# Four graph layers on one core: sixty edge columns listed at the first joint, three per relational group, twenty in a later node step

## The chip, the cores and the metric

One Trainium2 chip, one of its cores. The metric is the device time of one launch in microseconds, lower is better.

## What is computed

A graph of 3125 nodes with 128 features and 53125 directed edges, sorted by destination. Four layers follow each other, each wrapped as `x = layernorm(x + layer(x))`:

```python
# L0: five attention convolutions: per edge alpha = q[dst].k[src], softmax over the edges of one dst, sum of v[src]
# L1: one relational layer: softmax per (edge type, dst), sum of the weighted rows
# L2: two GCN layers: out = segment_sum(h[src] * dinv[src] * dinv[dst], dst) + b, elu between them
# L3: edge-weighted sum, and here the roles are turned round:
h = node_features @ weight
msg = edge_val[:, None] * h[edge_col]                     # edge_col is dst
out = jax.ops.segment_sum(msg, edge_row, num_segments=n)  # edge_row is src
```

The edges come sorted by destination, and L3 adds up by source. So the kernel must sort them once by source.

## The kernel before, in words

The edges are laid out as 416 columns of 128 (T = 416), in 13 groups (GROUPS) of 32 columns. Every edge pass goes through the groups in order. GpSimd (POOL) starts one indirect DMA per column, which fetches the rows of 128 edges from a table in DRAM (`gather_group`, L620), into one of two buffers per group parity. TensorE, VectorE and ScalarE work on the group before. A pass ends with a drain of some twelve turns, in which the other engines finish and POOL has no more gathers.

The passes in order: five attention convolutions (layers 0 to 4; layers 1 to 3 are one hardware loop), the relational pass (`rel_edges`), two GCN passes (`plain_edges`, tags g1_ and g2_) and the source-sorted pass (`list_edges`, tag s_). Between them stand node steps: `conv_next` (the joint behind layers 0 to 3), `last_joint` (behind layer 4), the block of n1 (`norm_joint`, behind the relational pass), the block of e1 (`elu_joint`, between the two degree passes g1 and g2) and that of n2. Each of these stages is a block: all engines leave it together, and the next begins.

**The edge list.** Layer 0's pass also ranks the edges by the block of their source. VectorE's last step (`placed`) gives each edge its place, and SP writes the places to DRAM (`ord_tab`, L973). From then on the list `lst_tab` can be filled: `order_in` (L627 and L628, two DMAs) loads some columns of places and of edge data (`ord_now`, `pay`), and `list_rows` (L634) starts one indirect DMA per column on POOL, which scatters 128 entries of 16 bytes. The 416 columns are spread over the program by hand, as `LISTED` says. Before the change:

```python
JOINT = 34; MID = 26; PER = MID + JOINT; DRAIN = 30; EACH = 6; BEHIND_REL = 50
LISTED = [JOINT + (CONVS - 2) * PER, DRAIN + 28, EACH * (GROUPS - 1), BEHIND_REL + 22]
```

So it lists 34 columns in the first joint, 26 in the drain and 34 in the joint of each of layers 1 to 3, 30 in the drain of layer 4 and 28 in the last joint, 6 behind the gathers of each of the first twelve relational groups, 50 behind the last relational gather and 22 in n1's block. The joints, the last joint and n1's block wait for the semaphore `listed`, that is until the entries have landed; the drains don't. Pass g2 loads the whole list (L2097).

Names used below. In the relational pass, VectorE's `leak` (L1750) is the first instruction that reads a gathered group: it waits for all 32 gathers of the group. `weigh` (L1724) is the last that reads the group's rows, and POOL may fill a buffer again when the `weigh` of the group two before is done.

Of the kernel before, what the change touches and what calls it, by code (L numbers as in the profile page):

```python
# [26 lines left out]
CONVS = 5  # L27
# [3 lines left out]
GROUPS = -(-EDGES // (P * TG))  # L31
T = GROUPS * TG
# [5 lines left out]
JOINT = 34  # L38
MID = 26
PER = MID + JOINT  # L40
DRAIN = 30
EACH = 6
BEHIND_REL = 50
LISTED = [JOINT + (CONVS - 2) * PER, DRAIN + 28, EACH * (GROUPS - 1), BEHIND_REL + 22]
MOST = 72
TW = 26
assert sum(LISTED) == T
NT = NPAD // P
# [4 lines left out]
def gnn_kernel(nc, xT_in, src_c, edges_c, dst_c, dst_row, prev_row, next_row, first_row, first_next, last_row,  # L53
# [14 lines left out]
    ord_tab = nc.dram_tensor("ord_tab", [P, T], i32).ap()  # L68
# [5 lines left out]
    def sem(name):  # L74
        if name not in sems:
            sems[name] = nc.alloc_semaphore(name)
        return sems[name]
# [11 lines left out]
    def settle(eng):  # L89

        eng.sem_inc(sem(f"settled_{eng.engine.name}"), 1)
# [22 lines left out]
    with root:  # L114
# [16 lines left out]
        ord_now = gsb("ord_now", [P, MOST], i32)  # L131
        pay = gsb("pay", [P, MOST, 4], i32)
# [492 lines left out]
        def order_in(eng, first, count, there="ord_in"):  # L625

            eng.dma_start(ord_now[:, 0:count], ord_tab[:, ds(first, count)]).then_inc(sem(there), 16)  # L627
            eng.dma_start(pay[:, 0:count, :], edges_c[:, ds(first, count), :]).then_inc(sem(there), 16)  # L628

        def list_rows(pool, count, since=0):  # L630


            for i in range(since, since + count):
                nc.gpsimd.indirect_dma_start(  # L634
                    lst_tab, bass.IndirectOffsetOnAxis(ap=ord_now[:, i:i + 1], axis=0), pay[:, i, :], None
                ).then_inc(sem("listed"), 16)
# [112 lines left out]
        def conv_next(l, nx, acc, sb, pb):  # L749
# [14 lines left out]
            with nc.Block() as block:  # L764
                @block.gpsimd
                def _(pool):
                    pool.wait_ge(sem("ord_in"), 32 * (l + 1))
                    settle(pool)
                    list_rows(pool, JOINT, 0 if isinstance(l, int) else MID)
                    pool.wait_ge(sem("listed"), 16 * PER * l + 16 * JOINT)  # L770
                    settle(pool)

                @block.sync
                def _(sp):
                    if isinstance(l, int):
                        order_in(sp, 0, JOINT)
                    store_rows(sp, l + 1, stage)

                @block.tensor
# [95 lines left out]
        def conv_edges(l, sb, pb, acc, deg=None, kv=None, fetch=None, nx=None, rank=None):  # L875
# [45 lines left out]
            with nc.Block() as block:  # L921
                @block.gpsimd
                def _(pool):
                    gather_all(pool, lambda g, par: gather_group(pool, tag, l, g, par, kv_tab, src_all, kv), since)
                    if rank is None:
                        pool.wait_ge(sem("ord_in"), 32 * (l + 1))
                        if not isinstance(l, int):
                            settle(pool)
                        list_rows(pool, MID if deg is None else DRAIN)

                @block.sync
                def _(sp):
                    def scatter_rows(g, par):
                        sp.dma_start(st8[:, par, :].bitcast(u8), st_tab[ds(g * P, P), :]).then_inc(sem(f"{tag}st_in{par}"), 16)

                    def sum_rows(g, par):
                        sp.dma_start(s8[:, par, :].bitcast(u8), s_tab[ds(g * P, P), :]).then_inc(sem(f"{tag}s_in{par}"), 16)

                    def group(g, par):
                        for q in range(QG):  # L940
                            n = quad(g, q)
                            at = bases(sp, g * TG + 4 * q)
                            if not skip(g):
                                sp.wait_ge(sem(tag + "qx"), n - QG + 1)
                                settle(sp)
                            for j in range(4):
                                sp.dma_start(qwin[:, q, j, :], q_tab[ds(at[j], P), :]
                                             ).then_inc(sem(f"{tag}qwin{q}"), 16)
                            if q == 1 and not skip(g):
                                if not (isinstance(g, int) and g < 3):  # L950
                                    sp.wait_ge(sem(tag + "S"), quad(g - 2, 0))
                                    settle(sp)
                                sum_rows(g - 1, 1 - par)
                            if q == 4 and not (isinstance(g, int) and g == LAST):
                                if not skip(g):
                                    sp.wait_ge(sem(tag + "ST"), quad(g, 0))
                                    settle(sp)
                                scatter_rows(g + 1, 1 - par)
                    scatter_rows(0, 0)
                    fetch(sp)  # L960
                    for g in range(3):
                        group(g, g % 2)
                    with sp.Fori(1, (GROUPS - 1) // 2 - 1) as k:
                        group(2 * k + 1, 1)
                        group(2 * k + 2, 0)
                    group(LAST - 1, 1)
                    group(LAST, 0)
                    sp.wait_ge(sem(tag + "S"), quad(LAST - 1, 0))
                    settle(sp)
                    sum_rows(LAST, 0)  # L970
                    if rank is not None:
                        sp.wait_ge(sem("k_placed"), 4)
                        sp.dma_start(ord_tab, r_i).then_inc(sem("k_out"), 16)  # L973
                        sp.wait_ge(sem("k_out"), 16)

                @block.tensor
                def _(pe):
# [266 lines left out]
        def conv_layer(l, name, nx, first=False):  # L1244
            with ExitStack() as keep:
                wide = maker(keep, nc.sbuf_tensor, name)
                kv = wide("kv", [P, 2 * TG, 2 * D]) if first else None
                if first:
                    with ExitStack() as part:
                        conv_project(nx, maker(part, nc.sbuf_tensor, name), maker(part, nc.psum_tensor, name))  # L1250
                    tables(kv)
                acc = wide("acc", [P, NPAD + P])

                def fetch(sp):
                    if not first:
                        order_in(sp, l * PER - MID, PER)
                    load_next(sp, l + 1, nx)
                    sp.dma_start(nx["ln"][:, :], col0[ds(l, 1), :, :].rearrange("l p n -> (l p) n")
                                 ).then_inc(sem("nx_cols"), 16)
                with ExitStack() as part:  # L1260
                    conv_edges(l, maker(part, nc.sbuf_tensor, name), maker(part, nc.psum_tensor, name), acc, None, kv, fetch, nx,
                               nx if first else None)
                with ExitStack() as part:
                    conv_next(l, nx, acc, maker(part, nc.sbuf_tensor, name + "_n"), maker(part, nc.psum_tensor, name + "_n"))
# [608 lines left out]
        def norm_joint(tag, acc, rs, sb, pb, loads, w, put, scale_n=None, pre=None, shift=None, aside=None, lists=False):  # L1873
# [17 lines left out]
            with nc.Block() as block:  # L1891
                if lists:
                    @block.gpsimd
                    def _(pool):
                        list_rows(pool, LISTED[3] - BEHIND_REL, BEHIND_REL)
                        pool.wait_ge(sem("listed"), 16 * T)

                @block.sync
                def _(sp):
# [274 lines left out]
        def elu_joint(tag, acc, y, w, bias, dinv_f, dinv_n, sb, pb):  # L2174
# [7 lines left out]
            stage = sb("stage", [P, 3, 4, D])  # L2182
            pp = [pb(f"pp{i}", [P, 4, D]) for i in range(4)]
            with nc.Block() as block:
                @block.sync
                def _(sp):
                    store_staged(sp, tag, stage, put_rows)
# [43 lines left out]
        def last_layers(dinv_f, dinv_n, rs):  # L2231
# [4 lines left out]
            with ExitStack() as keep:  # L2236
                wide = maker(keep, nc.sbuf_tensor, "_g")
                acc, y = wide("acc", [P, NPAD]), wide("y", [P, NPAD])
                wa, wb, wc = (wide(k, [P, D]) for k in ("wa", "wb", "wc"))
                bias = [wide(f"bias{i}", [P, 3]) for i in range(3)]  # L2240
# [7 lines left out]

                scope, sb, pb = part("g1_")
                with scope:  # L2250
                    plain_edges("g1_", CONVS + 1, acc, sb, pb, [(wa[:, :], w2[0]), (wb[:, :], w2[1]), (bias[0][:, :], b2[0])],
                                Head("g1_", acc, rs, diag, (wa, xT, dinv_f)))
                scope, sb, pb = part("e1_")
                with scope:
# [11 lines left out]
                scope, sb, pb = part("g2_")  # L2266
# [5 lines left out]
                scope, sb, pb = part("n2_")  # L2272
# [14 lines left out]
                scope, sb, pb = part("s_")  # L2287
                with scope:
                    list_edges(lst, dst_i, own, start_i, acc, sb, pb, Head("s_", acc, rs, diag))
                scope, sb, pb = part("n3_")  # L2290
# [127 lines left out]
        with ExitStack() as scope:  # L2418
# [3 lines left out]
            with ExitStack() as part:  # L2422
                deg = part.enter_context(nc.sbuf_tensor("deg", [1, NPAD + P], f32))
# [61 lines left out]
```

## Time and profile before

| | |
|---|---|
| median of 3 runs | 5692.46 us (5691.00 to 5696.89) |
| profiled execution | 5703.85 us, of which the span is 5702.0 us |
| busy share: PE, PEld, DVE, ACT, POOL | 64%, 51%, 59%, 27%, 71% |
| POOL instructions | 4168, of which 3744 gathers (L620) and 416 lists (L634) |
| mean granted TensorE clock | 0.689 of full speed |

Times in the rows are microseconds from the start of the span, durations in microseconds; the mean of a group is in ns. PE is TensorE's matmul, PEld its weight load, DVE VectorE, ACT ScalarE, POOL GpSimd, SP the DMA-issuing queue. A row of the timeline tells its start, its duration, the engine, the line, the operation, its output and inputs, and in brackets how long the engine was idle before and what ended that.

### The profile page before, as it was taken

To read this page: it belongs to the slowest core of one execution; us is meant where nothing else is said; L and a number is where in the kernel's file an instruction comes from. 1 tells how busy PE (TensorE), PEld (TensorE's weight loads), DVE (VectorE), ACT (ScalarE), POOL (GpSimd) and SP (SyncE) were. 2 spreads that over 40 slices of the span, in tenths; PEclk is the share of its full clock that TensorE was granted. 3 is DMA by queue.
4 is the path that set the end of the run, shared out by engine and by line. 5 is a ranking of instruction groups with operands and counts; after the bars stand their busy time and mean duration, and the time that the engine had idled before them with its cause. 6 is when DMAs were issued, how large, how long until landed. Compare 5 with 4: busy or idle time off the path is not lost. (4 is left out here: it accounts for less than half of the span.)

```text
span 5702.0 us, 84663 instructions
## 1 busy us (share of the span) xinstructions
PE 3639.0 (64%) x17936; PEld 2902.4 (51%) x17937; DVE 3386.0 (59%) x9194; ACT 1523.1 (27%) x3590; POOL 4073.0 (71%) x4168
## 2 busy tenths in 40 slices
PE   5767767666676756666888857777444444446556
PEld 3556546563565445654666546667333333343334
DVE  7777756665666646665666567777434343436665
ACT  4333324332343323332455522332100010000000
POOL 4477577776777777776777677777677767767775
PEclk6777777777677767776899955555655555557777
DMA  7656266554565275644656443331121121112111
GB/s 240 173 169 188 81 202 185 173 156 125 175 189 170 82 207 170 186 131 145 181 171 181 113 92 72 76 72 38 50 52 53 52 62 52 52 48 57 52 53 51
DMA packets 631577, 681.11 MB, mean 119 GB/s; under 512 B 178674, under 2 KB 512952, under 8 KB 631144
## 3 DMA queue, kind: packets, MB, share of 16 engines
q0 software_dynamic: 166480, 384.69, 24.2%
q1 hardware_dynamic: 464792, 293.16, 17.6%
q8 instruction: 93, 1.52, 0.1%
q14 instruction: 212, 1.74, 0.1%
HBM read 620.51 MB, written 56.89 MB: 119 GB/s over the span
## 5 line engine op out<-in xcount | busy, mean ns | idle before, releaser
L620 POOL DMA_INDIRECT kvconv<-kv_tab,src_all x1664 | 1627.2, 978 | 644.4 <-issue 498.5
L620 POOL DMA_INDIRECT rowsg_<-h_tab,src_all x832 | 789.8, 949 | 287.4 <-issue 252.9
L634 POOL DMA_INDIRECT lst_tab<-pay,ord_now x416 | 429.0, 1031 | 223.5 <-issue 124.6
L620 POOL DMA_INDIRECT rows_r<-rel_tab,idx_r x416 | 417.0, 1002 | 143.2 <-issue 123.4
L620 POOL DMA_INDIRECT rowss_<-h_tab,dst_i_g x416 | 398.3, 957 | 161.7 <-issue 121.9
L620 POOL DMA_INDIRECT kvlast<-kv_tab,src_all x416 | 410.0, 986 | 133.7 <-issue 121.9
L1063 ACT ACTIVATE Sconv<-s8conv 128x512 f32<-128x512 fp8e4 x384 | 240.8, 627 | 396.6 <-PE pA1conv L1021 288.8
L1125 DVE TENSOR_TENSOR msgconv<-kvconv,sm_attEconv 128x512 f32<-128x512 f32 x416 | 285.8, 687 | 84.0 <-PE pA1conv L1021 32.9
L1021 PEld LDWEIGHTS pA0conv<-Sconv,msgconv 128*128 128x128 f32 x1664 | 299.8, 254 | 13.5
L1021 PEld LDWEIGHTS pA1conv<-Sconv,msgconv 128*128 128x128 f32 x1664 | 290.4, 246 | 16.9
L1021 PE MATMUL pA0conv<-Sconv,msgconv 128*128 128x128 f32 x1664 | 298.5, 339 | 0.0
L1150 DVE TENSOR_REDUCE sm_alphaconv<-prodbconv 128x16 f32<-128x512 f32 x416 | 283.1, 681 | 2.4 <-DVE sm_exconv L473 0.5
L1021 PE MATMUL pA1conv<-Sconv,msgconv 128*128 128x128 f32 x1664 | 281.3, 326 | 0.0
L1053 ACT ACTIVATE STconv<-st8conv 128x512 f32<-128x512 fp8e4 x416 | 257.8, 628 | 84.1 <-DMA st8conv<-st_tab 79.0
L1609 PEld LDWEIGHTS pA_r<-S_r,msg_r 128*128 128x128 f32 x832 | 199.1, 329 | 9.4
L998 PE MATMUL pQ0conv<-qwinconv,STconv 128*128 128x128 f32 x832 | 146.8, 332 | 86.3 <-DMA qwinconv<-q_tab 84.2
L1609 PE MATMUL pA_r<-S_r,msg_r 128*128 128x128 f32 x832 | 199.0, 421 | 0.0
L2130 DVE TENSOR_SCALAR Sg_<-iota_row,rel_nowg_ 128x128 f32<-128x128 f32 x832 | 185.2, 315 | 9.3 <-DVE rel_nowg_ L641 4.8
L1616 PEld LDWEIGHTS pn_r<-last_now_r,msg_r 128*128 128x128 f32 x832 | 189.9, 333 | 0.0
L998 PEld LDWEIGHTS pQ0conv<-qwinconv,STconv 128*128 128x128 f32 x832 | 128.6, 235 | 106.2 <-DMA qwinconv<-q_tab 58.6
L998 PE MATMUL pQ3conv<-qwinconv,STconv 128*128 128x128 f32 x832 | 180.2, 388 | 2.1 <-ACT STconv L1053 1.1
L1616 PE MATMUL pn_r<-last_now_r,msg_r 128*128 128x4 f32 x832 | 177.5, 336 | 0.0
(655 smaller groups left out, 8961.6 us busy)
## 6 DMA issues: line engine op xcount, KB each, us to landing
qwinconv<-q_tab SPq DMA_DIRECT2D x1664, 64.0 KB
kvconv<-kv_tab,src_all POOLq DMA_INDIRECT x1664
st8conv<-st_tab SPq DMA_DIRECT2D x52, 512.0 KB
s8conv<-s_tab SPq DMA_DIRECT2D x52, 512.0 KB
qwinlast<-q_tab SPq DMA_DIRECT2D x416, 64.0 KB
kv_tab<-stageconv_n SPq DMA_DIRECT2D x28, 512.0 KB
rowsg_<-h_tab,src_all POOLq DMA_INDIRECT x832
q_tab<-stageconv_n SPq DMA_DIRECT2D x28, 256.0 KB
```

What stands on the lines that cost most here:

```text
L620: nc.gpsimd.indirect_dma_start(rows[:, par * TG + t, :], None, tab, bass.IndirectOffsetOnAxis(ap=idx[:, g * TG + t:g * TG + t + 1], axis=0 ...
L634: nc.gpsimd.indirect_dma_start(lst_tab, bass.IndirectOffsetOnAxis(ap=ord_now[:, i:i + 1], axis=0), pay[:, i, :], None).then_inc(sem("liste ...
L998: last = nc.tensor.matmul(pQ[q % RING][:, j, :], ST[:, q % 4, j * P:(j + 1) * P], qwin[:, q, j, :], start=True, stop=True)
L1021: last = nc.tensor.matmul(to, msg[:, q % 2, j, :], S[:, q % 2, j * P:(j + 1) * P], start=False, stop=j == 3)
L1053: nc.scalar.activation(ST[:, q % 4, :], st8[:, par, q * 4 * P:(q + 1) * 4 * P], ACT.Copy).then_inc(sem(tag + "ST"), 1)
L1063: nc.scalar.activation(S[:, q % 2, :], s8[:, par, q * 4 * P:(q + 1) * 4 * P], ACT.Copy).then_inc(sem(tag + "S"), 1)
L1125: v.tensor_tensor(heads(msg[:, q % 2, :, :]), heads(kv[:, s:s + 4, D:2 * D]), att.unsqueeze(3).to_broadcast([P, 4, H, HD]), ALU.mult).then ...
L1150: v.tensor_reduce(sm["alpha"][:, par, :, 4 * q:4 * q + 4].rearrange("p h t -> p t h"), prodb[:, :, :].rearrange("p t (h f) -> p t h f", h= ...
L1609: nc.tensor.matmul(to, msg[:, q % 4, j, :], S[:, q % 4, j * P:(j + 1) * P], start=False, stop=j == 3)
L1616: last = nc.tensor.matmul(pn[:, 0:R], msg[:, q % 4, j, :], last_now[:, par, t * R:(t + 1) * R], start=t == 0, stop=t == TG - 1)
L2130: last = v.tensor_scalar(S[:, q, j, :], iota_row[:, :], rel_now[:, t:t + 1], None, ALU.is_equal)
```

## The change

It redistributes the 416 columns. The list starts as soon as the places are in DRAM, in the drain of layer 0, with all 60 columns of a period loaded at once; the twelve relational groups take 3 each in place of 6; 62 columns go behind the relational gathers (50, then 12 in n1's block) in place of 72 (50 and 22); and 20 go into e1's block, loaded at the start of g1.

```diff
-EACH = 6
+EACH = 3
 BEHIND_REL = 50
-LISTED = [JOINT + (CONVS - 2) * PER, DRAIN + 28, EACH * (GROUPS - 1), BEHIND_REL + 22]
+LISTED = [(CONVS - 1) * PER, DRAIN + 28, EACH * (GROUPS - 1), BEHIND_REL + 12, 20]
...
                 def _(pool):
                     pool.wait_ge(sem("ord_in"), 32 * (l + 1))
                     settle(pool)
-                    list_rows(pool, JOINT, 0 if isinstance(l, int) else MID)
-                    pool.wait_ge(sem("listed"), 16 * PER * l + 16 * JOINT)
+                    list_rows(pool, JOINT, MID)
+                    pool.wait_ge(sem("listed"), 16 * PER * (l + 1))
...
                 def _(sp):
-                    if isinstance(l, int):
-                        order_in(sp, 0, JOINT)
                     store_rows(sp, l + 1, stage)
...
                     gather_all(pool, lambda g, par: gather_group(pool, tag, l, g, par, kv_tab, src_all, kv), since)
-                    if rank is None:
-                        pool.wait_ge(sem("ord_in"), 32 * (l + 1))
-                        if not isinstance(l, int):
-                            settle(pool)
-                        list_rows(pool, MID if deg is None else DRAIN)
+                    pool.wait_ge(sem("ord_in"), 32 * (l + 1))
+                    if not isinstance(l, int):
+                        settle(pool)
+                    list_rows(pool, MID if deg is None else DRAIN)
...
                         sp.dma_start(ord_tab, r_i).then_inc(sem("k_out"), 16)
                         sp.wait_ge(sem("k_out"), 16)
+                        order_in(sp, 0, PER)
...
                     if not first:
-                        order_in(sp, l * PER - MID, PER)
+                        order_in(sp, l * PER, PER)
...
                         list_rows(pool, LISTED[3] - BEHIND_REL, BEHIND_REL)
-                        pool.wait_ge(sem("listed"), 16 * T)
+                        pool.wait_ge(sem("listed"), 16 * sum(LISTED[:4]))
...
             pp = [pb(f"pp{i}", [P, 4, D]) for i in range(4)]
             with nc.Block() as block:
+                @block.gpsimd
+                def _(pool):
+                    list_rows(pool, LISTED[4])
+                    pool.wait_ge(sem("listed"), 16 * T)
+
...
-                    plain_edges("g1_", CONVS + 1, acc, sb, pb, [(wa[:, :], w2[0]), (wb[:, :], w2[1]), (bias[0][:, :], b2[0])],
+                    plain_edges("g1_", CONVS + 1, acc, sb, pb, [(wa[:, :], w2[0]), (wb[:, :], w2[1]), (bias[0][:, :], b2[0]),
+                                 (ord_now[:, 0:LISTED[4]], ord_tab[:, T - LISTED[4]:T]),
+                                 (pay[:, 0:LISTED[4], :], edges_c[:, T - LISTED[4]:T, :])],
                                 Head("g1_", acc, rs, diag, (wa, xT, dinv_f)))
```

## Rows read from the trace of the kernel before

**Rows 1.** the page's costliest groups: busy us, mean ns | idle before, its ender

```profile
L634 POOL DMA_INDIRECT lst_tab<-pay,ord_now x416 | 429.0, 1031 | 223.5 <-issue 124.6
```

**Rows 2.** busy us by stretch: PE, PEld, DVE, ACT, POOL; then clock, DMA share, GB/s

```profile
3676.00:3775.00 99.00, 73.94 (x382) 67.84 (x381) 73.31 (x226) 30.42 (x72) 75.83 (x77) 0.50 0.33 75
```

**Rows 3.** timeline, relational edges, GpSimd: start us, us, engine, line, op

```profile
3726.02 1.00 POOL L634 DMA_INDIRECT lst_tab<-pay,ord_now  x1 [0.30 <-issue]
...
3733.81 1.28 POOL L620 DMA_INDIRECT rows_r<-rel_tab,idx_r  x1 [0.30 <-issue]
...
3774.78 0.94 POOL L620 DMA_INDIRECT rows_r<-rel_tab,idx_r  x1 [0.30 <-issue]
```

**Rows 4.** waits of VectorE L1750 in the relational edges (us, times)

```profile
  DMA rows_r<-rel_tab,idx_r: 63.4, 12
```

**Rows 5.** timeline, relational edges, VectorE; in brackets the idle time before

```profile
3727.51 0.39 DVE L1750 TENSOR_TENSOR sm_alpha_r<-sm_alpha_r,rows_r 128x128 f32<-128x128 f32 x1 [6.09 <-DMA rows_r<-rel_tab,idx_r]
...
3731.16 0.39 DVE L641 CAST mask_now_r<-mask_r 128x384 f32 x1 [2.87 <-issue]
...
3777.56 0.39 DVE L1750 TENSOR_TENSOR sm_alpha_r<-sm_alpha_r,rows_r 128x128 f32<-128x128 f32 x1 [3.64 <-DMA rows_r<-rel_tab,idx_r]
...
3926.52 0.39 DVE L1750 TENSOR_TENSOR sm_alpha_r<-sm_alpha_r,rows_r 128x128 f32<-128x128 f32 x1 [8.71 <-DMA rows_r<-rel_tab,idx_r]
```

**Rows 6.** timeline, end of the relational edges

```profile
3991.41 0.59 ACT L1686 ACTIVATE acclast<-pA_r 128x511 f32 x1
3991.70 0.97 POOL L634 DMA_INDIRECT lst_tab<-pay,ord_now  x1 [0.30 <-issue]
```

**Rows 7.** timeline, first node step behind the relational edges (block of n1)

```profile
4002.63 0.97 POOL L634 DMA_INDIRECT lst_tab<-pay,ord_now  x1 [9.96 <-POOLq L1503]
...
4022.28 2.17 ACT L1966 ACTIVATE stage_n<-pp_n,sc_n 128x128 f32<-128x128 f32 x8
...
4029.39 0.97 POOL L634 DMA_INDIRECT lst_tab<-pay,ord_now  x1 [0.30 <-issue]
...
4035.03 0.35 SPq L2097 DMA_DIRECT2D wa_g<-in_w  x1
```

**Rows 8.** timeline, node step between the degree passes (block of e1)

```profile
4564.28 0.69 DVE L2222 TENSOR_TENSOR acc_g<-acc_g,dinv_f 128x512 f32<-128x512 f32 x1 [0.36 <-PEq L2089]
...
4582.04 1.14 ACT L2214 ACTIVATE stagee_<-pp2e_,dinv_n 128x128 f32<-128x128 f32 x4 [0.67 <-PE pp2e_ L2197]
...
4585.88 0.35 SPq L2097 DMA_DIRECT2D wc_g<-in_w  x1
4586.52 0.94 POOL L620 DMA_INDIRECT rowsg_<-h_tab,src_all  x1 [29.11 <-ACTq L2089]
```

**Rows 9.** transfers issued 645 to 660 us: KB, us to landing

```profile
ord_tab<-bkconv SPq DMA_DIRECT2D x1, 208.0 KB, 1.9
```

**Rows 10.** timeline, end of layer 0's edges and the first joint

```profile
652.14 0.35 SPq L973 DMA_DIRECT2D ord_tab<-bkconv  x1
...
685.10 0.59 ACT L1086 ACTIVATE accconv<-pA1conv 128x511 f32 x1
...
685.94 0.34 SPq L627 DMA_DIRECT2D ord_now<-ord_tab  x1
...
690.29 1.00 POOL L634 DMA_INDIRECT lst_tab<-pay,ord_now  x1 [43.21 <-DMA pay<-in_edges_c]
...
741.28 0.34 SPq L934 DMA_DIRECT2D st8conv<-st_tab  x1
```

**Rows 11.** timeline, the joint behind layer 3, first and behind its last instruction

```profile
2586.80 2.05 PE L799 MATMUL pc0conv_n<-accconv,centre 128*128 128x512 f32 x2 [4.66 <-PEq L921]
...
2639.85 0.35 SPq L934 DMA_DIRECT2D st8last<-st_tab  x1
```

**Rows 12.** timeline, last joint: a list instruction beside a VectorE instruction

```profile
3265.30 2.03 POOL L634 DMA_INDIRECT lst_tab<-pay,ord_now  x1 [0.31 <-issue]
...
3265.67 1.54 DVE L1429 TENSOR_SCALAR mask_r<-t_f_j 128x1248 bf16<-128x1248 f32 x1
```

## The prediction

> **What bounds the kernel now.** I first read the page for the engine with the highest share: POOL, 71%, with over four thousand indirect DMAs. Then the group of the list's own instructions [rows 1]: 416 of them, 1.031 us each, and the idle time before them is mostly "issue", which means that POOL waited for nothing. The question for each place where the change adds or takes away a list instruction is whether POOL sets the end there. That is read stage by stage.
>
> In the relational pass it does. In 99 us POOL is busy 75.8, VectorE 73.3 and TensorE 73.9 [rows 2], which is too close to decide by; the waits decide. POOL goes from the gathers of one group through its six lists to the next gathers with gaps of 0.30 and no semaphore [rows 3]. VectorE's first reader of a group, L1750, waits for the gathers in 12 of 13 groups, 63.4 us in all [rows 4], so 5.28 a group. POOL paces the pass, and VectorE has 5.28 us a group to spare.
>
> At the end of that pass two sides finish together: ScalarE at 3992.00 and POOL's fiftieth list at 3992.67 [rows 6]. In n1's block POOL is alone at the end: ScalarE is done at 4022.28 + 2.17 = 4024.45, the last list starts at 4029.39, and the next block begins at 4035.03 [rows 7]. In e1's block POOL does nothing, and the block lasts from 4564.28 to 4585.88 [rows 8]. In the drain of layer 0 POOL does nothing either, and ScalarE ends it at 685.69 [rows 10].
>
> **The price of one list.** From the first to the last of the 22 in n1's block there are 21 steps in 26.76 us, so 1.274 us each [rows 7]. The mean over all 416 is 1.031 busy [rows 1] plus the gap of 0.30 [rows 3], 1.335; the difference comes from single slow ones. I use 1.274 where the trace shows quiet lists and 1.335 in drains and joints.
>
> **Relational groups, 36 lists fewer.** 36 x 1.274 = 45.9 us, if POOL still paces the pass. Each group gets 3.82 us shorter, and the spare time is 5.28 on average, so 1.46 is left. Group by group it is tighter. From one L1750 at 3727.51 to the moment at which VectorE is ready for the next, 3777.56 - 3.64 = 3773.92, it needs 46.41 us, and in that stretch stands a stop of 2.87 that the loop's end costs it in every second group [rows 5]. POOL's period here is 50.05, and 46.23 behind the change. So VectorE comes 0.2 late in these groups and has 2.7 more in the next ones (without the 2.87 it needs 43.54), where it catches up. POOL is not held up by so little, because it waits only for the `weigh` of the group two before: a buffer has been read half a group before POOL comes to it. The last group has a wait of 8.71 [rows 5], so whatever VectorE was late by is gone when the drain begins. Bounds: 48.1 at the mean price of a list, 40.1 if VectorE needs 46.41 in every group (the mean period from 3727.51 to 3926.52 is 49.75 over four groups [rows 5]; 12 x 3.34). I take 45.9, since the lists beside these gathers are quiet: six of them take 7.79 us to the next gather, which is 1.30 each [rows 3]. TensorE runs at 0.50 of full speed there [rows 2], its 1.2 GHz level; it cannot fall further, and a rise would not shorten what POOL paces.
>
> Behind the last gather the count stays 50, so POOL's 3992.67 moves with the gathers. Loads get smaller (36 columns for 72, 62 for 72): nothing.
>
> **n1's block, 10 lists fewer.** The twelfth list starts at 4002.63 + 11 x 1.274 = 4016.6; from the last list to the next block it is 4035.03 - 4029.39 = 5.64 [rows 7], so the lists would allow 4022.3. The stores now set the end. In e1's block, where nothing else runs, 2.70 us pass from ScalarE's end to the next block (4583.18 to 4585.88 [rows 8]); 4024.45 + 2.70 = 4027.15. Gain 7.9.
>
> **e1's block, 20 lists more.** POOL's first instruction of a block comes 0.64 behind the block's first (4585.88, 4586.52 [rows 8]). So the lists begin at 4564.92, the twentieth at 4564.92 + 19 x 1.274 = 4589.1, and with the same 5.64 the next block begins at 4594.8 in place of 4585.88. Cost 8.9; below this it cannot fall, since POOL issues them in order. Nothing hides the excess: the next pass cannot gather before the block ends. Above: single lists that wait for VectorE. In the last joint a list took 2.03, 1.06 over the quiet 0.97, beside a tensor_scalar of 1.54 us [rows 12].
>
> The Trainium skill, page "SBUF — State Buffer", section "Who interferes with whom", speaks against this move: it says that VectorE's tensor_scalar can enter a mode in which it takes the port pair it shares with GpSimd, for the whole instruction, and GpSimd stands still. By that rule the trace of the last joint agrees. e1 has seven such instructions, one a block.
>
> I take none of it into the sum: e1's are 512 wide and the one in the row 1248, which would give 1.06 x 512 / 1248 = 0.43 for each that meets a list, 3.0 at most.
>
> **g1's start, two loads more.** TensorE waits for all loads of the pass. The same pair of loads took 4.35 from issue to POOL's go in the first joint (685.94 to 690.29 [rows 10]). It costs nothing: POOL begins with 64 gathers that wait for nobody, some 80 us, and TensorE and VectorE have slack behind them. Without that cover it would be 4.35.
>
> **Layer 0: drain and first joint.** SP writes the places at 652.14 [rows 10]; they land 1.9 later [rows 9], 654.0. The two loads, then POOL's go, 4.35: 658.4. 26 lists at 1.335: 693.1. The drain ended at 685.69 before and the joint began 0.25 later [rows 10]; now it begins 7.2 later (5.6 with quiet lists). In the joint the loads are gone from the start. It took 741.28 - 685.94 = 55.34 [rows 10], ending with the wait for lists that had begun late. The joint behind layer 3 has its columns loaded, lists the same 34, and takes 2639.85 - 2586.80 = 53.05 [rows 11]. 34 lists at 1.335 plus 0.64 and the wait are 51 to 52, so the stores set the end there. The joint saves 2.3. Sum: +4.9. Bounds: +1.0 (quiet lists, and the joint as short as its lists allow, 50.7) and +7.2 (the joint saves nothing). I take the joint behind layer 3, the nearest row.
>
> **Sum.** -45.9 - 7.9 + 8.9 + 4.9 = -40.0 us. The profiled execution took 5703.85, so 5663.8 of its kind; the median of the runs is 11.4 below that execution, and on it the sum gives 5652.5. A change of less than 0.2%, 11.4 us, is about what cannot be told from none here.
>
> **Rivals.**
> 1. VectorE becomes the bound of the relational pass: its slow groups are not made good in the others. For it: 46.41 against 46.23. Against it: 63.4 us of waits, of which only 45.9 are used. Gain 40.1 in place of 45.9: 5658.3.
> 2. VectorE holds up the lists in e1, as [rows 12] show it in the last joint: +3.0, 5655.5. By the rule of the Trainium skill named above this would be the likelier case.
> 3. Slower than before: the gathers are paced by their own delivery and not by POOL's issue, so that fewer lists between them bring no group sooner. Its place is the wait of L1750, its price the whole 45.9. What is left is +5.9: 5698.4. It decides when less than 5.9 of the 45.9 come back. Against it: the last gather of a group starts at 3774.78, and VectorE goes at 3777.56 [rows 3, 5], under 3 us later, and the DMA engines are busy a third of the time [rows 2].
> 4. The change does less than it says in the first joint, and its drain pays in full: +7.2 for +4.9, 5654.8.
>
> **How the numbers follow.** Forecast 0.75, rival 1 0.10, rival 2 0.08, rival 4 0.04, rival 3 0.03. The low end takes 48.1, 7.9, 8.9 and +1.0: -46.1, 5646. The high end takes 40.1, 7.9, 8.9 + 3.0 and +7.2: -28.9, 5663.6, so 5663. All cases but rival 3 lie more than 11.4 below the median, and rival 3 is within it or above: faster 0.96, same 0.03, slower 0.01.
>
> **What would show it.** Right: L1750's waits fall from 63.4 to about 18 and stay above zero in every second group; the twelve relational periods are 3.8 shorter; n1's block ends about 25 behind its first list and e1's block lasts 30.5; the last list is e1's twentieth, and the next block begins 5.6 behind its start; layer 0's joint begins near 693. Wrong: waits of POOL on `weigh` in the relational pass, L1750 without waits over several groups, or a period of 49.75 in spite of three lists.

## The result, and the profile after

The changed kernel takes 5669.98 us (median of 6 runs, 5662.05 to 5679.70), the kernel before on the same chip 5693.22 (6 runs, 5691.0 to 5702.89): ratio 0.9956, 95% interval 0.9945 to 0.9966, 23.2 us less. A later measurement (e13 below, 5 runs against 9) gave 5669.15 against 5697.72, ratio 0.9952 (0.9938 to 0.9965), 28.6 us less. The forecast was 40.0 less. So the direction was right and the size was not; both medians lie above the range's high end of 5663.

| | before | after |
|---|---|---|
| profiled execution (span) | 5703.85 (5702.0) | 5673.65 (5671.8) |
| POOL busy | 71% | 4076.9 us, 72% |
| mean granted clock | 0.689 | 0.692 |

The profiled executions differ by 30.2. The rest of the distance to 23.2 lies in where each stands among its own runs: before's is 10.6 above its median, after's 3.7. (The first interval, 0.9945 to 0.9966, is 19 to 31 us: it holds 28.6 and 30.2, and not 40.0.) The stages below are read from the profiled executions.

The group of the lists on the page of the changed kernel answers to [rows 1]: 416 as before, a little dearer each (1.042 for 1.031).

```profile
L634 POOL DMA_INDIRECT lst_tab<-pay,ord_now x416 | 433.5, 1042 | 207.4 <-issue 124.0
```

The stages, from the first gather's start to the last one's end, and the gaps between passes (us). The other stages were not touched; none of them moved by more than 2.1, and together they come to -0.2.

| stretch | before | after | change | forecast |
|---|---|---|---|---|
| layer 0's last gather to layer 1's first | 94.9 | 105.8 | +10.9 | +4.9 |
| 13 relational groups, first gather to last | 636.7 | 591.4 | -45.3 | -45.9 |
| last relational gather to n1's block | 78.5 | 78.4 | 0 | 0 |
| n1's block, to the start of the pass behind it | 33.1 | 27.6 | -5.5 | -7.9 |
| e1's block, first degree pass to second | 29.1 | 39.1 | +9.9 | +8.9 |

The big term held. VectorE's first reader of a relational group (L1748 here, L1750 before [rows 4]) now waits for the gathers in 2 groups of 13 in place of 12. The view is the changed kernel's line L1748 with what ended its waits:

```profile
L1748 DVE TENSOR_TENSOR sm_alpha_r<-sm_alpha_r,rows_r x13: 389/390/400, 3352.3 to 3893.5; 128x128 f32<-128x128 f32 x13
  DMA rows_r<-rel_tab,idx_r: 6.2, 2
```

The waits fell to 6.2 us, not to the 18 that I had forecast, and there are none over eleven groups, which the prediction had named as a sign of being wrong. As a sign it was badly chosen: VectorE has hardly anything to spare any more, yet POOL still sets the pace. Behind the first gather of the pass none of POOL's waits is longer than its usual 0.3, and from 3299.15 to 3850.10 twelve groups take 45.91 each, against the 46.23 of the forecast. The waits are shorter than forecast because VectorE's own time per group, from one L1748 to the next without the waits, is 44.6 in place of 43.6 before; why was not looked into.

The miss is in layer 0. Here are the last list of the drain, the first instructions of the joint on POOL and TensorE, and ScalarE's last one in the drain (timeline of the changed kernel; start, duration, engine, line, idle before):

```profile
658.49 0.99 POOL L634 DMA_INDIRECT lst_tab<-pay,ord_now  x1 [9.71 <-DMA pay<-in_edges_c]
692.07 0.97 POOL L634 DMA_INDIRECT lst_tab<-pay,ord_now  x1 [0.30 <-issue]
702.09 0.97 POOL L634 DMA_INDIRECT lst_tab<-pay,ord_now  x1 [9.04 <-POOLq L919]
701.39 1.19 PE L797 MATMUL pc0conv_n<-accconv,centre 128*128 128x512 f32 x1 [14.19 <-PEq L919]
687.59 0.59 ACT L1084 ACTIVATE accconv<-pA1conv 128x511 f32 x1
```

The first list starts at 658.49 (forecast 658.4) and the last ends at 693.04 (forecast 693.1). Then no engine does anything for 8.35 us, and the joint starts at 701.39. The forecast had it begin near 693, as soon as the lists were through. The view of the line at which the block ends (L919, `with nc.Block()`) shows what stands there. Columns: line, engine's queue, instruction, count, duration in ns as min/median/max, first and last start.

```profile
L919 SPq DRAIN  x1: 122/122/122, 656.6 to 656.6; - x1
L919 POOLq DRAIN  x1: 24132/24132/24132, 677.0 to 677.0; - x1
L919 DVEq DRAIN  x1: 1003/1003/1003, 684.9 to 684.9; - x1
L919 PEldq DRAIN  x1: 950/950/950, 686.3 to 686.3; - x1
L919 ACTq DRAIN  x1: 654/654/654, 687.6 to 687.6; - x1
L919 POOLq EVENT_SEMAPHORE  x2: 17/17/17, 701.2 to 701.2; - x2
```

Each engine leaves a block through a DRAIN. ScalarE's is over at 688.2. GpSimd's is reached by its queue at 677.0, while the lists are still being worked off, and lasts until 701.1, 8.1 us behind the last list. These records are in no list of busy time, so the idle time only says "POOLq L919". The same row of the kernel before (its line is L921):

```profile
L921 POOLq DRAIN  x1: 16076/16076/16076, 637.0 to 637.0; - x1
```

There it ends at 653.0, 5.9 us behind the last gather (647.09) and 33 us ahead of ScalarE's, so nothing hung on it.

### The profile page after: what moved, and what is told of

Its sections match the earlier page's. It is cut to its first block and busy times, and to the rows that moved or that the text cites. A ratio compares the mean times of both kernels' runs of the same rounds, so it can differ in the third digit from the quotient of the medians.

```text
span 5671.8 us, 84448 instructions
## 1 busy us (share of the span) xinstructions
PE 3587.7 (63%) x17715; PEld 2896.5 (51%) x17937; DVE 3388.0 (60%) x9194; ACT 1521.7 (27%) x3590; POOL 4076.9 (72%) x4168
## 5 line engine op out<-in xcount | busy, mean ns | idle before, releaser
L1019 PE MATMUL pA1conv<-Sconv,msgconv 128*128 128x128 f32 x1664 | 276.4, 321 | 13.8 <-issue 10.9
```

The lines of the kernel that those rows point to most:

```text
L1019: last = nc.tensor.matmul(to, msg[:, q % 2, j, :], S[:, q % 2, j * P:(j + 1) * P], start=False, stop=j == 3)
```

## The experiments

The experiments are numbered e1 to e15; the node step between the degree passes is always called e1's block here. On the chip of the first four, the kernel before took 5699.79 (5690.12 to 5705.43).

**e1, a wait for the lists ahead of layer 0's block end.** My first theory was that the gap came from list DMAs that were still outstanding.

```diff
                     list_rows(pool, MID if deg is None else DRAIN)
+                    if isinstance(l, int) and deg is None:
+                        pool.wait_ge(sem("listed"), 16 * MID)
```

> The changed kernel with one wait added: behind the 26 lists of layer 0's drain GpSimd waits until all of them are counted on `listed`, before its block ends. Theory A (a block that GpSimd leaves while its list DMAs are still outstanding ends about 9 us after the last of them, one that waits for them about 4.4 us after it, as 736.85 to 741.28 in the trace of before): the lists still end at about 693.05, the first joint begins at 697.5 instead of 701.4, and the run is 3.9 us under the changed kernel's. Rival B (the 8 to 9 us are what a block's end on GpSimd costs after any list, so a wait shortens nothing): first joint at 701.4, 0 us. Rival C (the wait is an extra step in front of the same end): 2 us slower.

Measured: 5671.42 (5665.66 to 5674.73), ratio 0.9950 (0.9937 to 0.9964). That is no gain over the changed kernel (0.9956 on its own chip). The last list ends at 693.27, and the joint starts at 702.94, 9.67 behind it in place of 8.35. Line L919 and the joint's first matmul in that trace:

```profile
L919 POOLq DRAIN  x1: 8062/8062/8062, 694.6 to 694.6; - x1
702.94 2.04 PE L797 MATMUL pc0conv_n<-accconv,centre 128*128 128x512 f32 x2 [15.52 <-PEq L919]
```

Theory A falls. The DRAIN begins at 694.6, when all lists have been counted, and still takes 8.06 us. The wait only moves it 1.3 later: rival C, smaller than its 2.

**e2 and e3, the same wait in all drains**, of the changed kernel and of the kernel before.

```diff
                     list_rows(pool, MID if deg is None else DRAIN)
+                    pool.wait_ge(sem("listed"), 16 * PER * l + 16 * (MID if deg is None else DRAIN))
+                    if not isinstance(l, int):
+                        settle(pool)
...
                     list_rows(pool, BEHIND_REL)
+                    pool.wait_ge(sem("listed"), 16 * (sum(LISTED[:3]) + BEHIND_REL))
```

The diff is e2's; in e3 the number waited for is smaller by 16 * MID, since layer 0's drain has no lists there.

> The changed kernel with that wait behind the drain's lists of all five graph layers and behind the 50 lists that the relational step's end issues. Theory A: layer 0 -3.9, layers 1 to 3 -4.6 each (ScalarE's last instruction of layer 2's drain ends at 1960.7, the block could end at 1961.2 instead of 1965.8), layer 4 nothing (its lists end 15 us before ScalarE does), relational step -4.9: together -22.6 against the changed kernel. Rival B: 0. Rival D (with GpSimd gone from the path the next engine is late: ScalarE's end plus the 2.70 us that stand between it and the next block at the end of e1's block): layers 1 to 3 only -2.4 each, together -16.

> The kernel before with the same waits (layer 0's drain has no lists there). Theory A: -13.8 for layers 1 to 3 and -4.9 for the relational step, -18.7 against the kernel before, so that two waits' worth of the change's own gain is to be had without moving a list; ratio 0.9967. Rival B: ratio 1.000. Rival D: -12, 0.9979.

Measured: e2 5677.49 (5673.75 to 5683.15), ratio 0.9960 (0.9946 to 0.9973), e3 5703.56 (5701.05 to 5713.41), ratio 1.0013 (1.0004 to 1.0022). None of the expectations held: both lose a little where a gain or nothing was expected (e3's loss is 0.1%). In e2 the five DRAINs of the layers last 8.06 to 9.03 us, although every list DMA has been counted before each:

```profile
L919 POOLq DRAIN  x5: 8057/8702/9028, 696.0 to 3237.6; - x5
```

So GpSimd's DRAIN does not wait for data. It has work of its own.

**e4, no lists in e1's block.**

```diff
-EACH = 3
+EACH = 4
-LISTED = [..., BEHIND_REL + 12, 20]
+LISTED = [..., BEHIND_REL + 20, 0]
...
```

GpSimd's part of e1's block and the two loads at the start of g1 go as well.

> The changed kernel with e1's 20 lists put back: 12 of them into the relational groups (four a group instead of three) and 8 into n1's block (20 behind the relational step's 50 instead of 12). By the traces, against the changed kernel: relational pass +12 x 1.274 = +15.3, n1's block +4 to +6 (at 22 lists it took 33.1 us, at 12 it took 27.6), e1's block -9.7 (from 31.3 to the 21.6 it had): +10 to +12. If the lists in e1 are held up by something that costs more than its own block shows, the sum is smaller than that: under +8. Against the kernel before: -24 lists in the relational pass -30.6, layer 0 +10.9 to +12.6, n1 -1 to -2: about -20.

Measured: 5678.52 (5674.64 to 5682.29), ratio 0.9962 (0.9949 to 0.9976): 21.3 under the kernel before, as expected. The changed kernel was not run in this set; e4 is 7.1 above e1 and 8.5 above the changed kernel on its own chip, less than the 10 to 12 and on both sides of the mark of 8 that the expectation set, so the time doesn't decide that question. The traces do: the relational groups take 607.5 for 591.4 (+16.1 for 12 lists), from the first degree pass to the second it takes 10.3 less, as the block's own +9.9 says, and the shortfall stands in n1's block, +3 in place of +4 to +6. From the last relational gather to the first of the source-sorted pass it is 1215.2 for 1221.7. The price of a list held.

**What the DRAIN's length hangs on.** GpSimd's DRAIN at the ends of the other blocks, from the traces at hand (four rows of the changed kernel, each the block's line, one of the kernel before):

```profile
L764 POOLq DRAIN  x4: 2821/2821/2821, 750.7 to 2649.6; - x4
L1288 POOLq DRAIN  x1: 2337/2337/2337, 3288.7 to 3288.7; - x1
L1889 POOLq DRAIN  x1: 1028/1028/1028, 3986.0 to 3986.0; - x1
L2182 POOLq DRAIN  x1: 1682/1682/1682, 4554.1 to 4554.1; - x1
```
```profile
L1891 POOLq DRAIN  x1: 1845/1845/1845, 4031.7 to 4031.7; - x1
```

All of these come behind a wait for the lists. Against the number of lists in their block: 12 took 1.028, 20 took 1.682, 22 took 1.845, 28 took 2.337, 34 took 2.821. That is a straight line, 0.05 us plus 0.0815 for each list since the last DRAIN; with none it takes 0.05 (e1's block of the kernel before, L2184). Behind 416 gathers and 26 lists it is 8.06, far less than 442 times that. Theory F said no more than that it stops growing somewhere. The traces say more, if one takes the end of the DRAIN less the end of the last instruction on GpSimd. Behind 416 gathers alone it is 5.94 in layer 0 of the kernel before and 6.59 in the degree passes, as much as 72 and 80 lists would take. Lists behind the gathers still count in full: 5.94 + 26 x 0.0815 is the 8.06 of layer 0, and in the other layers it is 8.55 with 24 lists (e15), 8.72 with 26 and 9.04 with 30. Only behind the relational groups does it flatten: 8.97 with 44 lists (e15) and 9.13 with 50.

Theory F says how to shorten layer 0's: run one DRAIN early, while GpSimd waits for the ordered table anyway.

**e5 to e8.** e5 puts one DRAIN on GpSimd there, e6 moves two lists of each layer from the drain to the joint, e7 moves six from behind the relational groups into n1's block, e8 does all three.

```diff
+                    if isinstance(l, int) and deg is None:
+                        nc.gpsimd.drain()
                     pool.wait_ge(sem("ord_in"), 32 * (l + 1))
...
-JOINT = 34
-MID = 26
+JOINT = 36
+MID = 24
...
-BEHIND_REL = 50
-LISTED = [..., BEHIND_REL + 12, 20]
+BEHIND_REL = 44
+LISTED = [..., BEHIND_REL + 18, 20]
```

> The changed kernel with one DRAIN instruction on GpSimd in layer 0, behind its 416 gathers and ahead of the wait for the ordered table, where GpSimd sits idle from 648.8 to 658.5. New theory F, from the DRAIN records at the blocks' ends (12 lists since the last DRAIN 1.028 us, 20 1.682, 28 2.337, 34 2.821; 8.06 in the first experiment for 26 lists behind 416 gathers): the DRAIN at a block's end takes 0.05 us plus 0.082 us for each indirect DMA issued since the last one, up to about 8 to 9 us, and a wait for the lists ahead of it does not shorten it. Then the early DRAIN is over at about 655 (it was over 6.0 us after the last gather before), the first list still starts at 658.5, the DRAIN at the block's end has 26 entries and 2.2 us of work in place of 8.1, and the first joint starts at 695.5 to 696.5 instead of 701.4: -5 to -6 in the layer. Rival G (the 8 us at the end belong to the lists' own landing or to the block): the joint still starts at 701.4, or later by what the added instruction takes: 0 or slower.

> The changed kernel with 24 lists in each drain and 36 in each joint of layers 0 to 3 instead of 26 and 34. Theory F with the DRAIN on the path: in layers 1 to 3 GpSimd's DRAIN ends at 1333.2 and 1965.5 where ScalarE's ends at 1330.0 and 1960.7, so two lists fewer start the joint 2.5 earlier in each; the joint's lists then end level with the last stores (3.1 us more work against 2.0 us of slack), costing 0.7: -1.8 a layer, in layer 0 nothing (lists follow each other through both blocks): -5 in all. Rival H (the block's end does not hang on GpSimd's DRAIN but on ScalarE plus 3.9 us): the joints start where they did, and the joints are longer by 0.7 each: +2.

> The changed kernel with 44 lists behind the relational groups and 18 in n1's block instead of 50 and 12. Theory F: GpSimd's DRAIN ends at 3968.7 and ScalarE's at 3959.0, so the six lists fewer end the block 6 x 1.274 = 7.6 us earlier; n1's block has 7.9 us between the end of GpSimd's DRAIN (3987.0) and of SyncE's (3994.9), so its six lists more, 6 x 1.36 = 8.1, cost 0.2: -7.4. Rival H: the relational block ends where it did, n1 +0.2: 0.

> The three edits together. Theory F: -5.5 (layer 0), -5 (layers 1 to 3) and -7.4 (relational step): -18 against the changed kernel, some 5652 to 5655, ratio to the kernel before about 0.9925. If the parts share the path (a saving in one stage given back in the next), less than the sum of the three single runs.

Measured: 7450.24, 7455.06, 7463.78 and 7454.29 us, ratios 0.9950, 0.9948, 0.9957 and 0.9945, where the kernel before took 7493.40 (7472.72 to 7522.45). On that chip the whole program takes a third longer, so these times tell nothing of the question. The four ratios can't be told apart, each interval being some 0.003 wide. The next set ran on such a chip again.

**e9 to e12, the same four kernels again.**

> The kernel of the fifth experiment again (one DRAIN on GpSimd behind layer 0's gathers), because on that chip the kernel before took 7493 us and the layer's end hung on ScalarE, so that a shorter DRAIN could not show in the time. Theory F (0.05 us plus 0.082 us for each indirect DMA since the last DRAIN, up to 8 to 9 us) on a chip on which before takes about 5700: GpSimd's last DRAIN in the layer ends 2.3 us after the 26th list instead of 8.1, the first joint starts at 695.5 to 696.5 instead of 701.4, and layer 1's first gather comes 5 to 6 us earlier than in the changed kernel; its time lies 5 us under that kernel's, ratio to before 0.9945 to 0.995. Rival G: the joint at 701.4.

> The kernel of the sixth experiment again, for the same reason. Theory F: joints of layers 1 to 3 start 2.5 us earlier after the last gather than in the changed kernel, and are up to 0.7 longer: -5 in all against the changed kernel. Rival H: they start where they did, +2 in all.

> The kernel of the seventh experiment again, for the same reason. Theory F: from the last relational gather to the start of n1's block 70.8 us instead of 78.4, n1's block 27.6 to 28.0 instead of 27.6: -7.4 against the changed kernel. Rival H: 78.4, and 0.

> The three edits together again. Theory F: -18 against the changed kernel, 5650 to 5655 where before takes about 5695, ratio about 0.9925. If a stage gives back what an earlier one saves, the sum of the three single runs is not reached.

Measured: 7527.99, 7522.39, 7534.90 and 7518.90, ratios 0.9953, 0.9949, 0.9958 and 0.9936, against 7562.78 (7535.44 to 7593.62) before. Inconclusive in time for the same reason. The traces still say two things. First, the DRAINs. Line of the added one (L924) and of the block's end (L919) in e9:

```profile
L924 POOLq DRAIN  x1: 11082/11082/11082, 843.8 to 843.8; - x1
L919 POOLq DRAIN  x1: 17503/17503/17503, 878.5 to 878.5; - x1
L919 ACTq DRAIN  x1: 654/654/654, 910.2 to 910.2; - x1
```

The early DRAIN is over at 854.8, 5.9 behind the last gather's end (848.90), and the late one at 896.0. ScalarE's ends at 910.9, so on this chip nothing in layer 0 hangs on GpSimd's. Second, why it is another program here: GpSimd's relational groups start at 4679.75 and 4748.49, 68.7 apart in place of 45.9, and in each of the last ten GpSimd waits four times for VectorE's `msg`, some 25 us in all. There GpSimd does not set the pace. Why VectorE is late on this chip stays open: for the waits of its own the trace only names a remote releaser. What the trace does show is that the short register steps between the instructions of VectorE and of SyncE are longer there: single ones take up to 1.4 us, where none takes over 0.2 in e14, which is the same kernel, and SyncE's MOVE has a mean of 0.135 us for 0.029. Those of TensorE, ScalarE and GpSimd are as long as in e14, and so are the lists.

**e13 to e15, one more set, on a chip where the kernel before takes 5697.72 (5690.39 to 5702.64).** e13 is the changed kernel as it is.

> The changed kernel as it is, as the base for the next two on the same chip. All theories: ratio to the kernel before 0.9945 to 0.9966 where before takes about 5695. Where before takes about 7500 a relational group is not paced by GpSimd (68 us a group in the traces of the last two calls against 46), so there the 36 lists fewer are worth nothing in the relational pass and what gain there is comes from elsewhere: ratio 0.995 to 1.000.

> The changed kernel with the early DRAIN in layer 0. Theory F: on a chip where before takes about 5695, first joint at 695.5 to 696.5 instead of 701.4 and 5 to 6 us under the changed kernel; where it takes 7500, no difference in time (ScalarE ends 4 to 14 us behind GpSimd there).

> All three edits. Theory F: 18 us under the changed kernel where before takes about 5695, of them 5.5 in layer 0, 5 in layers 1 to 3, 7.4 at the relational step's end. Rival: what one stage saves the next gives back, and the sum is under 12.

| | us | range of 5 runs | ratio to before (95%) |
|---|---|---|---|
| e13 changed kernel | 5669.15 | 5662.66 to 5675.96 | 0.9952 (0.9938 to 0.9965) |
| e14 early DRAIN | 5665.92 | 5659.93 to 5669.80 | 0.9943 (0.9930 to 0.9957) |
| e15 all three | 5656.87 | 5652.85 to 5662.32 | 0.9931 (0.9917 to 0.9944) |

Layer 0 in e13: the last list starts at 692.00, and the joint at 701.32.

```profile
692.00 0.97 POOL L634 DMA_INDIRECT lst_tab<-pay,ord_now  x1 [0.30 <-issue]
701.32 2.04 PE L797 MATMUL pc0conv_n<-accconv,centre 128*128 128x512 f32 x2 [13.09 <-PEq L919]
```

The same in e14, with both DRAINs of GpSimd:

```profile
L924 POOLq DRAIN  x1: 16271/16271/16271, 638.0 to 638.0; - x1
L919 POOLq DRAIN  x1: 17882/17882/17882, 676.5 to 676.5; - x1
691.17 0.96 POOL L634 DMA_INDIRECT lst_tab<-pay,ord_now  x1 [0.30 <-issue]
694.64 2.05 PE L797 MATMUL pc0conv_n<-accconv,centre 128*128 128x512 f32 x2 [8.51 <-PEq L919]
```

The early DRAIN ends at 654.3, before the ordered table is there, and delays nothing. The late one ends at 694.4, 2.2 behind the last list's end (692.14); the line for 26 entries says 2.17. The joint starts 2.5 behind the last list in place of 8.4, and from layer 0's last gather to layer 1's first it takes 99.8 in place of 105.8. So the DRAIN's 5.9 for the gathers are gone from the end of the block, rival G falls, and theory F holds in the time of the stage. In the medians it is 3.2, with overlapping ranges, too little to be told at five runs.

e15 is 12.3 under e13, and the two ranges don't touch. Expected were 18, and the rival said under 12, so it lies between the two; the profiled spans differ by 16.3 (5667.3 and 5651.0). By stage, against e13: layer 0's gap 105.8 to 100.1; from the last relational gather to the first degree pass 107.5 to 99.5; layers 1 to 3 together only 3.0 less (100.4, 102.1, 96.7 to 99.7, 99.6, 96.9) where 5 were expected. In the joints GpSimd is now last: its DRAIN for 36 lists ends at 1371.2, SyncE's at 1368.1. Whether moving one list in place of two keeps more was not run. The relational step's end, from e15 and from e13:

```profile
L1503 POOLq DRAIN  x1: 24405/24405/24405, 3922.2 to 3922.2; - x1
L1503 ACTq DRAIN  x1: 654/654/654, 3944.0 to 3944.0; - x1
L1891 POOLq DRAIN  x1: 1518/1518/1518, 3971.6 to 3971.6; - x1
L1891 SPq DRAIN  x1: 7/7/7, 3973.4 to 3973.4; - x1
```
```profile
L1501 POOLq DRAIN  x1: 24383/24383/24383, 3938.2 to 3938.2; - x1
L1501 ACTq DRAIN  x1: 654/654/654, 3952.1 to 3952.1; - x1
L1889 POOLq DRAIN  x1: 1028/1028/1028, 3979.7 to 3979.7; - x1
L1889 SPq DRAIN  x1: 7/7/7, 3989.4 to 3989.4; - x1
```

In e13 GpSimd's DRAIN ends at 3962.6 and ScalarE's at 3952.8: 9.8 us in which only GpSimd is at work. In e15 it is 3946.6 against 3944.7. n1's block takes the six lists (DRAIN 1.518 for 18, on the line) and still ends with SyncE. e15 is the best version of this study; by the medians it is faster than the kernel before by 0.7% and than the changed one by 0.2%.

## Why the prediction was wrong in size

- **Relational pass, -45.9: right.** -45.3 in the profile; e4 gives 16.1 for 12 lists. Rival 1 did not come true, but it is near: 2 waits are left of 12. Rival 3 (gathers paced by something else) did not happen on the chips where the kernel before takes 5700. On the slower ones GpSimd did not set the pace of this pass; what the whole change is worth there was not measured by itself.
- **Layer 0, +4.9: the step that failed.** The forecast said "The drain ended at 685.69 before and the joint began 0.25 later; now it begins 7.2 later". The lists ended where I had put them. But the 0.25 was ScalarE's way out of the block, and GpSimd's way out is another: a DRAIN of 8.1 us behind the last list. In the kernel before it was there as well and hidden, 33 us ahead of ScalarE's. The rows I had quoted showed it for two other blocks: TensorE idle for 4.66 at "PEq L921" before joint 3 [rows 11], and 9.96 of idle time at "POOLq L1503" between the fiftieth list and the next block [rows 7], which I carried along as a constant without asking what it was. For the same reason "two sides finish together" at the end of the relational pass was misread: ScalarE's DRAIN ends at 3992.0 and GpSimd's at 4001.7. The size of the failed term is larger than the miss of the stage. The joint began at 701.39 where I had 693.1, 8.3 late. In the stage 6.0 of it are left (10.9 in place of 4.9), because the last gather ended 1.7 later than in the kernel before, which shortens the gap behind it and has nothing to do with the change's lists, and because the joint saved 2.9 in place of 2.3. Of the DRAIN's 8.06, 5.9 stand for the gathers and 2.1 for the 26 lists; e14 takes the first part back and leaves the second. That 6.0 were missed and 6.0 came back is in part chance.
- **n1's block, -7.9: right in kind, the tail mis-sized.** It gave 5.5. ScalarE ended at 3992.37 and the next block began at 3996.52, 4.15 later; I had taken 2.70 from e1's block. Behind n1 stands `recycle()` with an empty block of its own, behind e1's block it does not. The kernel before ended its block by the lists, but both parts of the tail stand in its trace: SyncE's DRAIN ends 2.5 behind ScalarE, and the empty block and the clearing of semaphores take 1.3, from 4033.7 to 4035.03. The rest, 0.9, is ScalarE itself, which ended 23.44 behind the block's start in place of 22.50.
- **e1's block, +8.9: 9.7 in the block, 9.9 from pass to pass.** Two errors of mine partly cancel, by luck. The tail behind the lists took 3.2 in place of 4.7: the 5.64 that I carried over from n1's block hold the 1.3 of its clearing and empty block. And the lists took 27.4 us in place of 25.2. So VectorE does hold them up, as rival 2 says, but not with the instruction that it names. Rows of the changed kernel (GpSimd's lists and VectorE's instructions beside them):

```profile
4525.42 0.99 POOL L634 DMA_INDIRECT lst_tab<-pay,ord_now  x1 [7.74 <-POOLq L2087]
4530.63 1.42 POOL L634 DMA_INDIRECT lst_tab<-pay,ord_now  x1 [0.30 <-issue]
4532.36 1.42 POOL L634 DMA_INDIRECT lst_tab<-pay,ord_now  x1 [0.31 <-issue]
4535.80 1.25 POOL L634 DMA_INDIRECT lst_tab<-pay,ord_now  x1 [0.30 <-issue]
4537.35 0.97 POOL L634 DMA_INDIRECT lst_tab<-pay,ord_now  x1 [0.30 <-issue]
4539.90 1.47 POOL L634 DMA_INDIRECT lst_tab<-pay,ord_now  x1 [0.30 <-issue]
```
```profile
4525.51 0.49 DVE L2227 TENSOR_SCALAR lowe_<-acc_g,bias_g 128x512 f32<-128x512 f32 x1
4530.53 0.68 DVE L2225 TENSOR_TENSOR acc_g<-acc_g,dinv_f 128x512 f32<-128x512 f32 x1
4531.24 0.49 DVE L2227 TENSOR_SCALAR lowe_<-acc_g,bias_g 128x512 f32<-128x512 f32 x1
4532.25 0.68 DVE L2225 TENSOR_TENSOR acc_g<-acc_g,dinv_f 128x512 f32<-128x512 f32 x1
4535.51 0.69 DVE L2231 SCALAR_TENSOR_TENSOR y_g<-lowe_,y_g 128x512 f32<-128x512 f32 x1 [0.34 <-ACT lowe_ L2210]
4539.83 0.69 DVE L2231 SCALAR_TENSOR_TENSOR y_g<-lowe_,y_g 128x512 f32<-128x512 f32 x1 [1.47 <-ACT lowe_ L2210]
```

The first list has a tensor_scalar of 0.49 wholly inside it and takes 0.99, next to nothing above the quiet 0.97. The last has none and takes 1.47. What the slow ones share is an instruction of 0.68 with two inputs in SBUF that began just before them: begun 0.07 before, the list takes 0.50 longer, 0.11 before 0.45, and 0.29 before 0.28, that is, 0.56 less the head start. In four traces (the kernel before, the changed one, e13, e15) all 147 lists that start 0.03 to 0.5 behind such an instruction lie within 0.05 of this. The 103 that start as closely behind one with an input in PSUM (such as `prodbconv<-kvconv,pQ3conv`) take no more than 0.98. The forecast had 0.43 for each tensor_scalar as rival 2's price, seven times, and left it out of the sum; that the 3.0 come near the 2.2 is luck. The rule for tensor_scalar of the Trainium skill, page "SBUF — State Buffer", section "Who interferes with whom", is not what these rows show. The same section says that a VectorE instruction with two SBUF inputs contends with a GpSimd instruction that reads SBUF, and these traces agree. That should have been a term.
- **g1's loads and the relational drain, 0: right.** 521.7 to 520.5 and 78.5 to 78.4.
- **From the profile to the median.** The misses add up to 6.0 + 2.4 + 0.8 + 0.6 = 9.8, and 40.0 - 9.8 = 30.2 is what the profiled executions show; to the last tenth this is chance, since single stages that the change doesn't touch differ by up to 2 us between the two executions. The second measurement's 28.6 agrees with that. The first one's 23.2 is 5 to 7 less; with runs that scatter over 12 us before and 18 after, no stage has to answer for it.

The range was too narrow for the same reason: its high end priced layer 0 at +7.2, "the joint saves nothing", and left the way out of the block at next to nothing in every case.

## What to carry to other kernels

When a change makes an engine the last one in a block, its way out of the block is a new term; take it from a block which that same engine ended, and look up the DRAIN at the block's last line, which no busy time shows. For GpSimd with indirect DMAs it is no constant: one DRAIN in a stretch in which it idles anyway makes the later one short. And where one engine ends a block alone, as GpSimd did behind the relational groups by 9.8 us, compare all engines' DRAINs first: what can be moved from there is worth its full time, here without touching the pass that everybody looks at.

## What the runs showed of the hardware that was not expected

- GpSimd's DRAIN takes 0.05 us plus 0.0815 for each list DMA since the last DRAIN, on 12, 18, 20, 22, 28, 34 and 36 of them (1.028, 1.518, 1.682, 1.845, 2.337, 2.821, 2.984), and the same within 7 ns, for all but 22, on the chips on which the program took 7500 us. A pass of 416 gathers adds 5.9 or 6.5 to that and not 34.
- All DMAs having landed does not shorten it; a wait ahead of it makes the block's end 1.3 us later (e1). That the time goes into clearing one record of each DMA is my reading of the straight line and was not shown.
- A list DMA on GpSimd that starts within half a microsecond behind a VectorE instruction of 0.68 us with two SBUF inputs takes up to 0.5 longer (1.47 for 0.97), and not behind one with an input in PSUM.
- Some chips run the same program in 7500 us in place of 5700, with the same lengths of the lists and DRAINs, with longer register steps on VectorE and SyncE, and with waits of VectorE for a remote releaser. Differences of a few us in GpSimd's path can't be measured there in the time.
